# A two-layer network on one core: new orders of stages for four engines, one list per engine over all four pairs, and a new table of PSUM banks

## What is computed

```python
# layer 0, attention: kernel features of q and k, per head
qp = softmax_kernel(q, proj, is_query=True)     # exp(xp - diag - rowmax) + eps
kp = softmax_kernel(k, proj, is_query=False)    # exp(xp - diag - max over all tokens) + eps
out = einsum(qp, einsum(kp, v)) / einsum(qp, sum(kp))
x = layer_norm(video + out @ Wo.T); x = layer_norm(x + relu(x @ W1.T) @ W2.T)
# layer 0, feed-forward: the top expert's low-rank addition before the relu
y = relu(x @ wi.T + lora_of_top_expert(x)) @ wo.T
# layer 1, attention: 16 heads, the tokens in 8 chunks of 64, one after the other
def step((W, b), (xq, xk, xv)):
    Z1 = xk @ W + b;  x_hat = normalized(Z1)
    grad_x = gradient of the layer norm at (g * x_hat + be - (xv - xk))
    W, b = W - (eta * xk).T @ grad_x, b - sum(eta * grad_x)
    return (W, b), xq + g * normalized(xq @ W + b) + be
# layer 1, feed-forward: token shift, r = sigmoid(xr @ Wr), out = r * (relu(xk @ Wk)**2 @ Wv)
```

## Time and profile before

| | us |
|---|---|
| median of 3 runs | 1005.95 (1004.88 to 1006.24) |
| profiled execution: span, first to last instruction | 1004.5 |
| lowest of the runs shown less that span | 0.4 |
| median of the runs less that span | 1.45 |
| PE busy | 949.1 (94%) |
| DVE busy | 787.3 (78%) |
| ACT busy | 651.5 (65%) |
| POOL busy | 343.0 (34%) |
| mean granted clock of TensorE | 0.977 |
| instructions | 26971 |

### The profile page before, as it was taken

One profiled execution on the slowest core, in us unless ns is written; L12 is line 12 of the kernel. 1 busy time (PEld: TensorE's weight loads), 2 busy tenths in 40 slices (PEclk: granted clock), 3 DMA queues, 4 the chain that ended last, 5 costly groups with the idle time before them and its releaser, 6 DMA issues.

```text
span 1004.5 us, 26971 instructions
## 1 busy us (share of the span) xinstructions
PE 949.1 (94%) x10906; PEld 714.9 (71%) x10906; DVE 787.3 (78%) x1945; ACT 651.5 (65%) x1240; POOL 343.0 (34%) x456
## 2 busy tenths in 40 slices
PE   7788899999999999999999999899999998999995
PEld 5565575778787766787887776677787775777773
DVE  5856359988799679968888769987889847888973
ACT  2642274897856575888666566689765556686762
POOL 1992011343341321333242222143341323454450
PEclk9799999999999999979999989999999989999998
DMA  9000010000000010000000010000000000000000
GB/s 333 14 1 1 11 33 1 2 2 2 3 1 3 22 32 1 3 1 3 2 13 1 12 43 2 2 2 2 2 12 2 12 23 2 2 2 13 2 2 21
DMA packets 15831, 16.14 MB, mean 16 GB/s; under 512 B 2013, under 2 KB 14301, under 8 KB 15325
## 3 DMA queue, kind: packets, MB, share of 16 engines
q1 hardware_dynamic: 15709, 14.43, 4.7%
HBM read 10.23 MB, written 2.10 MB: 12 GB/s over the span
## 4 chain that ended last, share of the span: by engine, by line
PE 62%; DVE 24%; ACT 6%; issue 4%; POOL 3%; DMA 0%; DVEq 0%; ACTq 0%; POOLq 0%; SPq 0%
PE ps L546 8%; PE ps L607 4%; PE ps L539 4%; PE ps L631 4%; PE ps L590 3%; PE ps L601 3%; PE ps L528 3%; PE ps L490 3%; PE ps L613 3%; PE ps L520 3%; PE ps L521 3%; PE ps L499 2%; POOL gbase L1316 2%; DVE kmax L1004 2%; DVE tmp L1110 2%
## 5 line engine op out<-in xcount | busy, mean ns | idle before, releaser
L1316 POOL TENSOR_TENSOR gbase<-zhat,gamma 128x512 f32<-128x512 f32 x64 | 81.2, 1269 | 395.1 <-DVE scl L1104 388.5
L1324 POOL TENSOR_TENSOR zq_sqq<-zq_sqq,qinv 128x512 f32<-128x512 f32 x64 | 68.1, 1069 | 185.1 <-DVE qinv L1127 185.1
L780 ACT COPY w_sb<-ps 65x1024 f32<-65x1024 f32 x72 | 72.6, 1008 | 15.6 <-PE ps L607 12.1
L546 PEld LDWEIGHTS ps<-w_sb,keys 65*64 65x64 f32 x2048 | 66.0, 139 | 18.6 <-issue 10.9
L546 PE MATMUL ps<-w_sb,keys 65*64 65x64 f32 x2048 | 73.8, 226 | 3.8 <-ACT zT L835 1.5
L607 PE MATMUL ps<-grad,k_sc 64*65 64x64 f32 x2048 | 74.4, 222 | 2.6 <-DVE grad L1121 2.3
L607 PEld LDWEIGHTS ps<-grad,k_sc 64*65 64x65 f32 x2048 | 66.0, 135 | 14.8 <-issue 12.5
L1107 DVE TENSOR_TENSOR gbase<-gbase,ps 128x512 f32<-128x512 f32 x64 | 43.6, 681 | 40.7 <-POOL gbase L1316 29.3
L546 PEld LDWEIGHTS ps<-w_sb,queries 65*64 65x64 f32 x2048 | 66.2, 140 | 11.5 <-issue 5.4
L613 PEld LDWEIGHTS ps<-h,pack_ttt 128*128 128x128 f32 x512 | 64.5, 194 | 12.8 <-issue 6.6
L546 PE MATMUL ps<-w_sb,queries 65*64 65x64 f32 x2048 | 73.1, 226 | 0.3 <-ACT queries L788 0.2
(11 more groups left out here) (247 smaller groups left out, 2370.9 us busy)
## 6 DMA issues: line engine op xcount, KB each, us to landing
x<-in_x SPq DMA_DIRECT2D x8, 256.0 KB, 3.4
xc<-x SPq DMA_DIRECT2D x16, 128.0 KB, 2.4
out_x<-xc SPq DMA_DIRECT2D x16, 128.0 KB, 2.4
pack_ttt<-in_ttt SPq DMA_DIRECT2D x1, 1216.0 KB
keys<-in_gam_bet_rows SPq DMA_DIRECT2D x1, 1024.0 KB
w_sb<-in_compose SPq DMA_DIRECT2D x1, 1024.0 KB, 10.5
pack_expert<-in_expert SPq DMA_DIRECT2D x1, 792.0 KB, 16.8
zq_sqq<-in_wmod SPq DMA_DIRECT2D x1, 768.0 KB, 4.5
```

The source lines that it names most:

```text
L546: last = mm(bank[b][64 * c:64 * c + 64, (h % HH) * HD:(h % HH + 1) * HD], src[:, h, 64 * c:64 * c + 64], w_sb[:, f, c, h % HH, :], start=T ...
L780: nc.scalar.copy(w_sb[:, f, :, :, :].rearrange("p b h d -> p (b h d)"), ps[0:C, 2 * f:2 * f + 2, :].rearrange("p a c -> p (a c)")).then_in ...
L1316: P.tensor_tensor(gbase[:, cols], zhat[:, cols], gamma2[:, cols], ALU.mult).then_inc(S["g_hat"], 1)
L1324: P.tensor_tensor(heads(zq_hat[:, cols]), heads(zq_hat[:, cols]), per_head(qinv[:, hs]), ALU.mult).then_inc(S["zq_ready"], 1)
```

## The change

`ORDERS` has one string for each engine over all four pairs in place of three, so that pairs 0, 1 and 2 no longer share one order. The strings and the bank table are new. PE's wait for layer 1's weights and for POOL's setup stood in stage `r` of pair 0 and now stands ahead of the first layer 1 stage, whichever that is; it is `r` of pair 0 in the new string as well. Each engine runs the same instructions on the same data as before, but for the table loads on ACT, which follow from the order: 33 before, 34 now. The line numbers fall by 13 in PE's part and by 10 in the parts of ACT, DVE and POOL.

```diff
 ORDERS = {
-    "PE": (("011011100011000111011011001010110010110100100010"),
-        ("rkskls1a00q1lb0nakqn0kbld1aedl1eabk1bqd0lkfqfaed0lqea1kbqlob0d1fk0eafqbnodnlk111ae1fb1kq1dl0aed10lbfk0aed0qbo0"
...
+    "PE": "100111100011001101011011001010100111100100100010rs1kkls0a0l1qb0akq0dklb1ale1dkbea1qd0bkqflelq1dafaekboqk1b1l0df0feaqol"
...
-BANKS = ("01234567023541670237023541670416273501462735014627350146273501462735014627530146275346754675465764756454756475"
...
+BANKS = ("0123456712345067145206371542016542370615423706154327065143270651432703651427036514270365476574565674564674567457465745"
...
 def turns(engine):
 
-    first, middle, last = ORDERS[engine]
     taken = dict.fromkeys(PER_TOKEN, 0)
-    for what in first + middle.replace("n", "") + (PAIRS - 2) * middle.replace("n", "m") + last:
+    for what in ORDERS[engine]:
         pair, step = divmod(taken[what], PER_TOKEN[what])
         taken[what] += 1
-        if pair < PAIRS:
-            yield what, pair, step
+        yield what, pair, step
...
+            layer1_set = False
             for what, p, step in turns("PE"):
                 if what in "01":
                     layer0(p, step, int(what))
-                elif what == "r":
-                    if p == 0:
-                        loaded(pe, "ttt")
-                        pe.wait_ge(pool_set, N_POOL_SET)
+                    continue
+                if not layer1_set:
+                    loaded(pe, "ttt")
+                    pe.wait_ge(pool_set, N_POOL_SET)
+                    layer1_set = True
+                if what == "r":
                     start(p)
```

More of the change, by code:

```diff
@@ L115 @@
-    "DVE": (("110110010100101010111101010100010111100010110000"),
-        ("r0n101nazbca0z0bc1aezy1beaczy1bc0a0nze1yaebczy0b1aczb101ecyaez111b1cy0az01e0bcyaz0be01c0ayzbcena0zybcmaey0z10m"
-          "0ebca0zye101b0yam1czbc0e011eayzbyc0m1eeyny11m"),
-        ("rmmazbaczbcazeybcazeybcazebcamyzebcmayzebcayzebcayzebcamzyebcayzbcazebcyazebcyazemybceamyzebcaeyyzbceymmeymmmm"
-          "mm")),
-    "POOL": ((""),
-        ("zzzzyyzyzyzooyzyzyzyzzoyoyzozyzyyzyyyooo"),
-        ("zzzyzyzyzyzyzoyzzyyzozoyzoyzyyzoyyzyyooo")),
-}
@@ new lines @@
+    "ACT": ("011101101100001101101101010010011101100100010010s1rk0lka0vsql10akvqdkl1a1lvede0kaw1vqw0dkqflledaqwvfaevw0kkoq1df1lf0ea"
+            "1ovlqwd1k1aev1f0ldkqa0vw1ed0qlf10w1avekd1klfoewavqld0w10fa0kveq0ol0dwmfaevd0qfkmoklew0qavl0dkf0q1w0ela10wv1fqd1oave1wq"
+            "d10dfewewfomf10fm1orm0kslm0akv1slqm1a0vmkldk11aevqdlewak1vq00ldkwqefalvwdfqaewv0qfok1kd1lf1eao1vlmdq1wka0ev10dkl0fa11v"
+            "qwe0wd1fkl0qa0lved1kfowqlaevd1few0a0vokw0ld0avkfqmqk0fdle0amweoqv00wldfkq1e0al1v0wdmf11qea1qwvd1mf0doefewwof10fm1orkm0"
+            "slkmqa10vls0a1qvmkld1aevk1wdl0eak1vlqw0kdfeflaqvdwqaev0mko11qldwa0fvmkeqf1kol1d1awv10l10edfqakvw1e01dwlk01afevqdlkofma"
+            "0e0wvqwld0k1fleav0odqq0fewkavwldq0fea0kvoq0mf0dl1we0ka101vfwoqdlmae1vm1dfwq1df0eeww01off1mkslroavmklsqmavkdlkaqvemdlwq"
+            "kaevlmdwfqekalvwqdfkavoeldqwekalvfdwmkfaveqlmdwqoakvlfdkfalevwdeqkqalvdofawevkqwfldekawovldqfeakqvlwdfekfoawmveldqfwaq"
+            "evwommdfqfewdefwmfmoommmmm"),
@@ new lines @@
+    "DVE": ("0111101001001011000111011100100011110100011010001r100azbca0z0bca1ez1bcaezyy1bc10eayzaezbc1y0b10caez11yba1cz01bc00eaz1y"
+            "be0c1y1a1zebc0a0yze0bca0zbyc0meayezm0bc00ayzm100eyb1cea1zbm1ycae1z1b00ycee0yy11mr0m01maz1bca0z0bca1ez1beayczm1bcyaez0a"
+            "e1zyym0bc1b0caze11bc01yaz11bc0ea1zy10eby0c1a0z0beycaz0beca0zebycm1yazm000be0aycemzy100b1az0ce1bcy10meamzyb1ce0ey1y11mr"
+            "0m10maz1b0acz0bca1ze1ybcaez1y0bcea1zmaye0zbcb0az0my11cbe11c1ayz1bc0ea1z1yeb01yc0a01z0becaze0yb0cayz0mebmcaezy0b0a0ceyz"
+            "101a0by1cm0ezb1y1c0aze1bcymm0eyey11rmazmbcazmbcazebcayzeybcaezmbayczebcayzebcaymzebcyazbcaezmbcyazebayezcbyceazybcaezy"
+            "mbecayzmebycaeyzbceymmeymmmmmm"),
```

31 lines of the change are left out of this document (16 added, 15 removed).

## The result

The change made the kernel slower. Its median is **1033.69 us** (1032.98 to 1038.11, 4 runs) against 1005.41 us (995.91 to 1006.24, 4 runs), a ratio of **1.0321 [1.0279, 1.0364]**. I had forecast 1002.6 us and a range that ended at 1009. The profiled execution has a span of 1031.7 us.

A forecast was written before the change was run, and what follows sets the result against it. PE's work and waits bound the kernel, with DVE sharing the limit in places. Terms -2.5 - 2.2 + 1.1 + 0.3 = -3.3 took the span from 1004.5 to 1001.2; plus 1.45 for the median, 1002.6 us, range 993 to 1009.

The forecast's parts named there:

- step (2): Pair 3, slots 2 to 15: DVE waits less for POOL's product between z and b; -2.2 us, ends 0 and -3.5.
- (3): Opening of pair 3: m5 and m6 now inside the first two slots, PE's steps shifted; +1.1 us, ends 0 and +3.
- (5): Everything else (pair 0's layer 0, tail, bank table, transfers, added wait check, POOL's list): put at 0.
- Step (1): Q_SHIFT to d5, pairs 0 to 2: gain of 5.0 us if DVE alone sets the length, else 0; half taken, -2.5.
- Step (4): ACT in pair 2: one more table load of 1.28 us, between 0 and 1.3; +0.3 us taken.
- larger gain: Rival, chance 0.20: smaller PE waits no longer lower the clock at 425 and 650 us; 6.75 us more gain, 995.9 us.
- slower rival: Rival, chance 0.22: ACT becomes the bound mid-kernel, exponentials hold PE's state copy in pairs 0 to 2; 7.5 us, 1010.
- The sentence on what would make me wrong: Wrong if time moves mainly where PE was full before, in the middle of a pair, or in layer 0 of pair 0.

The follow-up runs named there:

- extra-product runs: Kernel before with one or two more POOL products, read by nobody, behind each of its 64 steps z: 1020.6 us with one, 1091.2 us with two.

## Why the prediction was wrong

**The step that failed is the ground of the whole sum: "since no instruction is altered, only waits and the clock can change".** The same instructions took DVE 36.5 us more, and with most of POOL's work cut away they took the same time in both orders (771.2 and 771.1 us) and some 20 of the 23.4 us of full-speed time were gone. The sum had no term for it.

**In step (2) it stands as "a mixing step or a `c` 0".** I priced a stage between z and b by the wait that it covers and gave it no cost. The waits came out as predicted, from 11.6 us to

```profile
DVE gbase L1097 <- POOL gbase L1306: 7.5, 8, 1.4
```

where I had said about 7. But the stages that fill them are those that can't run beside POOL: m6 of pair 2 took 1.7 us longer, m7 1.7, m9 1.3, m1 of pair 3 1.6. The waits shrank by 4.1 us and these four stages grew by 6.3, so what I booked as -2.2 is nothing or a little worse. Pair 3 lost 2.4 us from a0 to the end where (2) and (3) together said -1.1. For the opening itself (3) was a little too dark: a0 to d0 takes 10.8 us as before, and a0 to d1 0.65 more at full speed, where I took 1.1.

**The same error in (5), "The rest I put at 0"**, cost far more: of the 37 us by which the stretching grew, 7 lie in pair 3 and 30 ahead of it. Putting two-source or SBUF-to-SBUF stages behind z was done in pairs 0 to 2 as well, and c now runs beside more of POOL's y and o. I looked at POOL's list only for POOL's own load, "POOL is busy 60.0 of 128.6 us even in pair 3", and took an engine that is far from full to be harmless. Its busy time was the wrong number to read; which DVE instructions run at the same moment was the right one. The kernel before had the sign of it: L1099 and L1153 have steady means, but L1115's mean is 756 ns where the instructions of its kind that run with POOL idle take 691.

**Step (1), -2.5**, failed in large part by the same cause. The stretch from Q_SHIFT to d5 in pairs 1 and 2 takes 62.8 and 66.7 us, both at a clock of 1.00. Before it took 63.1 and 60.0, or 58.1 and 58.2 at full speed (63.1 x 0.92, 60.0 x 0.97). That is 4.7 and 8.5 us longer, with 2.1 and 3.2 us of PE's work moved in. I took half of a gain that needs DVE to have the same work at the same price, and in pair 1 DVE was busy 60.87 us in place of 57.26, which is what the stretching grew by (3.6 us). In pair 2 stretching is 4.5 of the 8.5 us; DVE also has more work there than the z6 that I had counted, namely b6 and one more layer 0 step.

**Step (4), +0.3**: ACT has its 34 loads, each 1283 ns. Nothing in the runs speaks for or against its size.

**The rivals.** The larger gain's condition came true, both falls of the clock went away, and its conclusion did not: others came, at 0.70 from 125 to 150 us and 0.86 from 200 to 225, and two in pair 3; the mean is 0.974 for 0.977. I had also overlooked two falls of 6.8 us each in the kernel before, at 589 and 821 us. And the 2 us that I took for what can be told apart were too few for a time that spreads over 15 us. The slower rival had the right sign and the wrong mechanism: PE waited 1.5 us in all for ACT's copy of the state. I had given all that is slower 0.22 and named one engine for it, the one that is nearly full in one stretch; no rival of mine held that instructions could change their length. The sentence on what would make me wrong held: the time went mainly in the first three pairs.

What stays open: the 20 us that need POOL are shown as a sum. How they divide between stages held at the lock and what these then delay was not measured, and the extra-product runs mix in a late y. The 3.6 us of plain order were not followed further. I did not change DVE's list alone over whole pairs, nor the bank table alone.
